# Inverting the softmax sums in three sets of chunks, and storing the last attention output in the final stage

## The chip, the cores and the metric

The kernel runs on one core of a Trainium2 chip. The metric is the device time of one execution in microseconds, as the median of several runs. Engines are named TensorE (PE in the profile, PEld for its weight loads), VectorE (DVE), ScalarE (ACT), GpSimd (POOL) and SyncE (SP). SPq, ACTq and POOLq are the DMAs that an engine issues.

## The reference

x has 2 sequences of 2048 tokens with 256 channels; everything is float32, with 16 heads of 16 channels.

```
x = x + attn_a(layernorm(x))   # 44 fixed offsets per token, local
x = x + ffn(layernorm(x))      # 8 groups of 512 tokens, each its own W1, b1, W2, b2
x = x + attn_b(layernorm(x))   # rotary positions, softmax over all 2048 tokens
x = x + ffn(layernorm(x))      # the same weights again

# attn_b, the part that the change touches
attn = softmax(einsum('bqhd,bkhd->bhqk', q, k) * DH ** -0.5)
out = einsum('bhqk,bkhd->bqhd', attn, v).reshape(b, l, d)
return out @ Wo
```

## The kernel before

The program has three stages, each a block of its own: all five engines have to arrive at the end of one before any goes on to the next. `local_stage` does attn_a, the first feed-forward and the projections of attn_b. `full_attention` does the softmax attention. `final_stage` does the output projection, the second feed-forward and the stores.

**full_attention** goes over 2 sequences, 4 groups of 4 heads and 4 query chunks of 512 tokens, 32 iterations in all (y = 0 to 31, chunks innermost). In each, TensorE makes the scores of 16 key tiles (L1270), ScalarE their exponentials (L1343), and TensorE weighs the values (L1279) into one PSUM bank: for each head 16 rows of unscaled output and one row with the sum of the exponentials. TensorE also makes the scores of the next iteration once more so that VectorE can take row maxima (L1241, L1357); the negated maxima go through SyncE into extra rows of the query tile (`neg_rows`, L1145), and TensorE waits for them at the start of an iteration. The last iteration has no next one, so VectorE has no work of this kind in it.

ScalarE copies the finished bank to the tile `ou` (`take_output`, L1333), a few exponentials into the next iteration. SyncE stores it with 8 DMAs (`output`, L1151 and L1152): per head 16 rows to `o_d`, and the row of sums to `s_d`. The softmax isn't divided here. That is done per chunk c of 512 tokens over all heads (c = 0 to 7; 0 to 3 are the first sequence, 4 to 7 the second; the last head group of the second sequence finishes chunks 4 to 7 in iterations 28 to 31):

- `load_totals` (L1046, 4 DMAs) and `load_outputs` (L1053, 4 DMAs) bring the sums and outputs of chunk c back to SBUF. GpSimd issues them for chunks 0 to 6 once the stores of that chunk have landed, and with them `load_rest` (x, the feed-forward's weights, a bias). Chunks 0 to 3 come while the last head group runs.
- `invert` (L1067): VectorE takes the reciprocals of the sums.
- `store_inverse` (L1073): SyncE stores them, 4 DMAs a chunk, to `r_d`.
- `load_inverse` (L1079): SyncE loads them again, each row spread over 16 partitions, 2 DMAs of 256 KB a chunk.
- `divide` (L1088): VectorE multiplies a chunk's output by them.

For chunks 0 to 6 the sums, outputs, inverse stores and inverse loads each have one semaphore, and its waits ask for all seven chunks. So VectorE inverts nothing until chunk 6's sums are there, SyncE loads nothing until all 28 stores have landed, and VectorE divides nothing until all 14 loads have. Divides 0 to 5 are the last of VectorE's work in the stage, divide 6 stands in the final stage. SyncE's order at the end of the stage is: output 30, stores of chunks 0 to 6, loads of chunks 0 to 6, output 31.

**final_stage** goes over the chunks. For each, TensorE projects (L1502), VectorE adds x (L1553), a layer norm follows in five steps over three engines (L1425 to L1466), then the feed-forward matmuls (L1512; its two layers were folded into one matrix earlier), VectorE's update (L1561) and ScalarE's store (L1537). SyncE fetches chunk 7 here: it waits for all outputs, then loads sums and outputs, stores and loads the inverse. VectorE inverts chunk 7 while it works on chunk 1 and divides it while it works on chunk 3.

## Time and profile before

| | us |
|---|---|
| median of 3 runs | 2459.34 |
| the runs | 2453.56, 2459.34, 2460.16 |
| the profiled execution's own time | 2459.12 |
| its span | 2457.4 |
| TensorE busy in the span | 2325.7 |
| VectorE busy | 1933.8 |
| ScalarE busy | 1590.6 |
| TensorE's mean granted clock | 0.978 of full speed |

Times in the trace count from the start of the span. The full attention runs from about 878 to 2345 us, the final stage from 2363 to the end. A fp32 matmul over 512 columns shows as two instructions. A line in the profile may be that of a helper that many places call (L1046 serves GpSimd and SyncE alike), so engine and tile have to be read with it; `ks` and `qs`, the key and query tiles, hold the chunks' buffers once attention no longer needs them. DMA issues aren't counted as busy time.

### The profile page before, as it was taken

Reading aid. Unit: us, or ns where it says so; the run is one execution under the profiler, and the core shown is the slowest. Engines: PE = TensorE matmul, PEld = TensorE weight load, DVE = VectorE, ACT = ScalarE, POOL = GpSimd, SP = SyncE. Lnnn points to the kernel's source line nnn. Section 1 sums busy time; section 2 is a strip of 40 time slices with the busy share of each in tenths; the row PEclk is TensorE's granted clock in tenths of the full one; section 3 lists DMA queues with packets and bytes.
Section 4 is the critical chain, followed back from the end, with each engine's and each line's share of the span. In section 5 each row is a group of like instructions: output and inputs, shape, how many; then the busy total and the mean of one; then the engine's idle time right before and its main releaser. Section 6 shows DMA issues by size and latency. Waiting matters only on the chain. (4 is left out here: it accounts for less than half of the span.)

```text
span 2457.4 us, 49260 instructions
## 1 busy us (share of the span) xinstructions
PE 2325.7 (95%) x14912; PEld 907.6 (37%) x14912; DVE 1933.8 (79%) x2283; ACT 1590.6 (65%) x3672; POOL 779.8 (32%) x1020
## 2 busy tenths in 40 slices
PE   7899999999987779999999999999999999999968
PEld 5455555555544322232323333333323232323223
DVE  4877988898867677888888888888888888888346
ACT  0356676766653156777777777777777777777821
POOL 2788988898871034020020020020000000041200
PEclk9999999999998799999999999999999999999989
DMA  8355545565566079050050050050000000030221
GB/s 268 114 130 126 159 119 151 136 152 136 149 139 151 14 133 107 7 71 3 4 71 3 4 71 4 3 71 4 3 20 5 2 20 5 2 108 27 64 98 52
DMA packets 246488, 178.42 MB, mean 73 GB/s; under 512 B 107238, under 2 KB 216118, under 8 KB 246374
## 3 DMA queue, kind: packets, MB, share of 16 engines
q1 hardware_dynamic: 210428, 114.37, 18.2%
q0 software_dynamic: 16480, 43.52, 11.3%
q10 hardware_dynamic: 19472, 19.12, 2.4%
q8 instruction: 63, 1.03, 0.2%
q14 instruction: 45, 0.37, 0.1%
HBM read 119.86 MB, written 48.31 MB: 68 GB/s over the span
## 5 line engine op out<-in xcount | busy, mean ns | idle before, releaser
L1343 ACT ACTIVATE pr<-ps_s 128x512 f32<-128x512 f32 x2048 | 1114.2, 598 | 338.5 <-PE ps_s L1270 314.4
L1357 DVE TENSOR_REDUCE mx<-ps_m 128x1 f32<-128x1024 f32 x980 | 1153.8, 1219 | 223.8 <-PE ps_m L1241 217.6
L1270 PE MATMUL ps_s<-qs,ks 99*128 (+1 forms) x2048 | 702.2, 383 | 20.2 <-SPq L1136 7.6
L1241 PE MATMUL ps_m<-ks,qs 96*128 (+1 forms) x1960 | 586.3, 380 | 0.0
L1279 PE MATMUL ps_o<-pr,vg 128*32 128x512 f32 x4096 | 546.3, 605 | 0.7 <-DMA vg<-vb_d 0.5
L541 POOL TENSOR_TENSOR qs<-ks 128x512 f32<-128x512 f32 x336 | 428.0, 1307 | 70.0 <-ACT ks L792 43.6
L1270 PEld LDWEIGHTS ps_s<-qs,ks 99*128 (+1 forms) x2048 | 195.6, 96 | 654.0 <-issue 429.6
L1184 POOL DMA_DIRECT2D vg<-vb_d x24 | 19.6, 817 | 1172.9 <-PE ps_o L1279 1085.0
L1241 PEld LDWEIGHTS ps_m<-ks,qs 96*128 (+1 forms) x1960 | 189.9, 98 | 173.6 <-issue 10.1
L871 DVE TENSOR_TENSOR ks<-PSa,ks 128x512 f32<-128x512 f32 x368 | 232.3, 677 | 22.6 <-PE PSa L626 20.4
L626 PE MATMUL PSa<-ks,sj 128*32 128x512 f32 x736 | 198.8, 608 | 4.7 <-issue 2.7
L626 PE MATMUL PSa<-qs,sj 128*32 128x512 f32 x672 | 198.7, 606 | 1.5 <-POOL qs L541 1.5
L1279 PEld LDWEIGHTS ps_o<-pr,vg 128*32 128x32 f32 x4096 | 80.6, 108 | 207.3 <-ACT pr L1343 155.6
L815 ACT ACTIVATE attn<-PSa,red 128x44 f32<-128x44 f32 x416 | 117.5, 314 | 6.4 <-DVE red L937 6.1
L822 ACT COPY qs<-PSa 128x512 f32<-128x512 f32 x128 | 69.4, 600 | 45.9 <-PE PSa L694 38.6
L815 ACT ACTIVATION_READ_ACCUMULATOR attn<-PSa,red 128x1 f32 x416 | 92.7, 223 | 0.0
L1177 POOL DMA_DIRECT2D qs<-q_d x168 | 85.6, 513 | 16.1 <-issue 5.1
L694 PE MATMUL PSa<-ident,qs 128*128 128x128 f32 x512 | 70.2, 281 | 12.9 <-DMA qs<-skew 9.6
L591 PE MATMUL PSa<-tail_room 128*128 128x256 f32 x256 | 65.5, 412 | 12.7 <-DMA tail_room<-in_W2T 9.3
L694 PEld LDWEIGHTS PSa<-ident,qs 128*128 128x128 f32 x512 | 57.7, 143 | 46.9 <-issue 35.7
L631 PE MATMUL PSa<-t_xm,wqkv_b 128*128 128x512 f32 x128 | 61.6, 626 | 5.5 <-DVE ks L977 5.0
L556 POOL TENSOR_TENSOR far<-far,fart 128x128 f32<-128x128 f32 x128 | 63.0, 492 | 10.0
(190 smaller groups left out, 2147.5 us busy)
## 6 DMA issues: line engine op xcount, KB each, us to landing
qs<-skew SPq DMA_DIRECT2D x64, 512.0 KB
ks<-k_d POOLq DMA_DIRECT2D x48, 256.0 KB, 8.9
qs<-q_d POOLq DMA_DIRECT2D x180, 64.0 KB, 9.1
skew<-attn SPq DMA_DIRECT2D x64, 164.0 KB, 4.7
tail_room<-in_W SPq DMA_DIRECT2D x32, 256.0 KB, 3.3
tail_room<-in_W2T SPq DMA_DIRECT2D x32, 256.0 KB, 4.1
vb_d<-vb SPq DMA_DIRECT2D x8, 1024.0 KB, 6.6
q_d<-qparts ACTq DMA_DIRECT2D x16, 384.0 KB, 2.7
```

The source lines that it names most:

```text
L541: pool.tensor_tensor(prod_p[:, n % RING, :], qT[:, c, :], kT[:, c, col:col + CH], ALU.mult).then_inc(prod_p_ready, 1)
L626: pe.matmul(PS[SLOT * g:SLOT * (g + 1), SC_BANK, :], sj[:, BANK_J * bank + 4 * g + r, :], rhs[:, n % RING, :], start=(r == 0), stop=(r == ...
L694: tr = pe.transpose(PS[:, TURN_BANK[half], h * P:(h + 1) * P], own[:, w % 2, 4 * half + h, :], ident[:, :])
L815: ex = act.activation(attn[:, w % 2, h, :], logits[:, h, :], ACT.Exp, bias=red[:, w % 2, 0, h:h + 1], accum_out=red[:, w % 2, 1, h:h + 1])
L822: act.copy(a0[:, 4 * half:4 * half + 4, :], PS[:, TURN_BANK[half], :].rearrange("p (h t) -> p h t", h=4)).then_inc(turn_sb, 1)
L871: dve.tensor_tensor(prod_d[:, n % RING, :], PS[:, Q_BANK[c], :], kT[:, c, col:col + CH], ALU.mult).then_inc(prod_d_ready, 1)
L1177: pool.dma_start(qs[r, bass.ds(g * NCH + n, 1), :, :].rearrange("p a j t -> p (a j) t"), D["q_d"][Q_STACK[i], :, heads, bass.ds(b * T + (1 ...
L1241: mm = pe.matmul(ps_m[:, u % 2, kc * CH:(kc + 1) * CH], qs[0:KROWS, bass.ds(nq, 1), j, qt * P:(qt + 1) * P].rearrange("p a t -> p (a t)"), ...
L1270: pe.matmul(ps_s[:, op % SB, :], ks[0:KROWS + PARTS, bass.ds(slot, 1), j, kt * P:(kt + 1) * P].rearrange("p a t -> p (a t)"), qs[0:KROWS + ...
L1279: mm = pe.matmul(ps_o[SLOT * j:SLOT * (j + 1), :], vg[:, kt, j, :], pr[:, kt % 4, j, :], start=(kt == 0), stop=(kt == KT - 1), skip_group_ ...
L1343: act.activation(pr[:, kt % 4, j, :], ps_s[:, op % SB, :], ACT.Exp, scale=HD ** -0.5).then_inc(p_ready, 1)
L1357: dve.tensor_reduce(mx[:, j * TILES + qt, half:half + 1], ps_m[:, u % 2, :], AX_X, ALU.max).then_inc(m_read, 1)
```

## The change

The chunks fall into three sets, 0 to 3, 4 to 6, and 7. Sums loaded, outputs loaded, inverses stored and inverses loaded have a semaphore for each set, and each wait asks for its own set. VectorE's order becomes: invert 0 to 3, divide 0 to 3, invert 4 to 6, divide 4 to 6, all in the attention stage; divide 6 is no longer in the final stage. SyncE's order becomes: the last `neg_rows`, stores of chunks 0 to 3, their loads, output 30, stores of chunks 4 to 6, their loads. Output 31 moves behind the stage boundary and is the first thing that SyncE does in the final stage. For that, `output` is now a function of the module, and `ou` and its semaphore are among the final buffers. GpSimd's program and the arithmetic are as before.

```diff
--- before.py
+++ after.py
@@ -998,6 +998,8 @@
 
 
 EARLY = 2
+SET_SIZE = (NCH, NCH - 1, 1)
+SET = [0] * NCH + [1] * (NCH - 1) + [2]
 
 
 def final_buffers(nc, ctx, A):
@@ -1009,6 +1011,7 @@
         "spread": sb("spread", [P, TILES, P]),
         "eps": sb("eps", [P, 1]),
         "wo": sb("wo", [P, KC, C]),
+        "ou": sb("ou", [P, CH]),
     }
     own = {
         "xc": sb("xc", [P, EARLY, KC, CH]),
@@ -1034,21 +1037,32 @@
         F["total"].append(own["total"][:, c] if c < EARLY else place(c % 2, P))
         F["inv"].append(place(c % 2, KC * CH).rearrange("p (k t) -> p k t", k=KC))
     F["bcc"] = [own["bcc"][:, c] for c in range(NG)]
-    for n in ("const_ld", "wo_ld", "filled", "total_ld", "o_ld", "last_total_ld", "last_o_ld", "x_ld", "inverse_ready", "inverse_stored",
-              "inverse_ld", "o_ready", "o_stored"):
+    for n in ("const_ld", "wo_ld", "filled", "x_ld", "inverse_ready", "o_ready", "o_sb", "o_stored"):
         F[n] = sem(n)
+    for n in ("total_ld", "o_ld", "inverse_stored", "inverse_ld"):
+        F[n] = [sem(n + str(k)) for k in range(len(SET_SIZE))]
     return F
 
 
+def output(sp, D, F, y):
+    ou = F["ou"]
+    sp.wait_ge(F["o_sb"], y + 1)
+    for j in range(GRP):
+        first = SLOT * j
+        sp.dma_start(D["o_d"][y, HD * j:HD * (j + 1), :], ou[first:first + HD, :]).then_inc(F["o_stored"], 16)
+        sp.dma_start(D["s_d"][y // (HG * NCH), y // NCH % HG, y % NCH, :, j, :],
+                     ou[first + HD:first + HD + 1, :].rearrange("p (q t) -> p q t", q=TILES)).then_inc(F["o_stored"], 16)
+
+
 def load_totals(eng, D, F, c):
-    loaded = F["total_ld"] if c < NG - 1 else F["last_total_ld"]
+    loaded = F["total_ld"][SET[c]]
     for q in range(TILES):
         eng.dma_start(F["total"][c][SLOT * q:SLOT * q + H, :], D["s_d"][c // NCH, :, c % NCH, q]).then_inc(loaded, 16)
 
 
 def load_outputs(eng, D, F, c):
     b, n = c // NCH, c % NCH
-    loaded = F["o_ld"] if c < NG - 1 else F["last_o_ld"]
+    loaded = F["o_ld"][SET[c]]
     for g in range(HG):
         eng.dma_start(F["oT"][c][64 * (g % 2):64 * (g % 2) + 64, g // 2, :], D["o_d"][(b * HG + g) * NCH + n]).then_inc(loaded, 16)
 
@@ -1060,31 +1074,26 @@
 
 
 def invert(dve, F, c):
-    if c < NG - 1:
-        dve.wait_ge(F["total_ld"], 16 * TILES * (NG - 1))
-    else:
-        dve.wait_ge(F["last_total_ld"], 16 * TILES)
+    dve.wait_ge(F["total_ld"][SET[c]], 16 * TILES * SET_SIZE[SET[c]])
     dve.reciprocal(F["total"][c], F["total"][c]).then_inc(F["inverse_ready"], 1)
 
 
 def store_inverse(sp, D, F, c):
     sp.wait_ge(F["inverse_ready"], c + 1)
     for q in range(TILES):
-        sp.dma_start(D["r_d"][c, :, q * P:(q + 1) * P], F["total"][c][SLOT * q:SLOT * q + H, :]).then_inc(F["inverse_stored"], 16)
+        sp.dma_start(D["r_d"][c, :, q * P:(q + 1) * P], F["total"][c][SLOT * q:SLOT * q + H, :]).then_inc(F["inverse_stored"][SET[c]], 16)
 
 
 def load_inverse(sp, D, F, c):
+    sp.wait_ge(F["inverse_stored"][SET[c]], 16 * TILES * SET_SIZE[SET[c]])
     for k in range(KC):
         src = D["r_d"][c, 8 * k:8 * k + 8, :].unsqueeze(1).broadcast_to([8, HD, CH])
-        sp.dma_start(F["inv"][c][:, k, :], src).then_inc(F["inverse_ld"], 16)
+        sp.dma_start(F["inv"][c][:, k, :], src).then_inc(F["inverse_ld"][SET[c]], 16)
 
 
 def divide(dve, F, c):
-    dve.wait_ge(F["inverse_ld"], 16 * KC * (NG - 1 if c < NG - 1 else NG))
-    if c < NG - 1:
-        dve.wait_ge(F["o_ld"], 16 * HG * (NG - 1))
-    else:
-        dve.wait_ge(F["last_o_ld"], 16 * HG)
+    dve.wait_ge(F["inverse_ld"][SET[c]], 16 * KC * SET_SIZE[SET[c]])
+    dve.wait_ge(F["o_ld"][SET[c]], 16 * HG * SET_SIZE[SET[c]])
     dve.tensor_tensor(F["oT"][c], F["oT"][c], F["inv"][c], ALU.mult).then_inc(F["o_ready"], 1)
 
 
@@ -1114,13 +1123,12 @@
         vg = sb("vg", [P, KT, GRP, SLOT], F32)
         pr = sb("pr", [P, 4, GRP, CH], F32)
         mx = sb("mx", [P, GRP * TILES, HALVES], F32)
-        ou = sb("ou", [P, CH], F32)
         q0_ld, first_max = sem("c_q0_ld"), sem("c_first_max")
         (qk_ld, qk_ready, va_ld, vb_ld, vc_ld, s_ps, p_ready, pv_done, m_ps, m_read, nm_step,
-         nmp_ready, nmt_ps, nmt_sb, neg_ld, o_sb) = (sem("c_" + n) for n in (
+         nmp_ready, nmt_ps, nmt_sb, neg_ld) = (sem("c_" + n) for n in (
              "qk_ld", "qk_ready", "va_ld", "vb_ld", "vc_ld", "s_ps", "p_ready", "pv_done", "m_ps",
-             "m_read", "nm_step", "nmp_ready", "nmt_ps", "nmt_sb", "neg_ld", "o_sb"))
-        o_stored = F["o_stored"]
+             "m_read", "nm_step", "nmp_ready", "nmt_ps", "nmt_sb", "neg_ld"))
+        ou, o_sb, o_stored = F["ou"], F["o_sb"], F["o_stored"]
         block = ctx.enter_context(nc.Block())
 
         def unit_place(u):
@@ -1144,25 +1152,19 @@
                 sp.wait_ge(nmt_sb, y + 1)
                 sp.dma_start(qs[KROWS:KROWS + PARTS, y % (HG * NCH), :, :].rearrange("a j t -> a (j t)"), nmt[:, :]).then_inc(neg_ld, 16)
 
-            def output(y):
-                sp.wait_ge(o_sb, y + 1)
-                for j in range(GRP):
-                    first = SLOT * j
-                    sp.dma_start(D["o_d"][y, HD * j:HD * (j + 1), :], ou[first:first + HD, :]).then_inc(o_stored, 16)
-                    sp.dma_start(D["s_d"][y // (HG * NCH), y // NCH % HG, y % NCH, :, j, :],
-                                 ou[first + HD:first + HD + 1, :].rearrange("p (q t) -> p q t", q=TILES)).then_inc(o_stored, 16)
-
             neg_rows(1)
             for x in range(2, ITERS):
-                output(x - 2)
+                output(sp, D, F, x - 2)
                 neg_rows(x)
-            output(ITERS - 2)
-            for c in range(NG - 1):
+            for c in range(NCH):
                 store_inverse(sp, D, F, c)
-            sp.wait_ge(F["inverse_stored"], 16 * TILES * (NG - 1))
-            for c in range(NG - 1):
+            for c in range(NCH):
                 load_inverse(sp, D, F, c)
-            output(ITERS - 1)
+            output(sp, D, F, ITERS - 2)
+            for c in range(NCH, NG - 1):
+                store_inverse(sp, D, F, c)
+            for c in range(NCH, NG - 1):
+                load_inverse(sp, D, F, c)
 
         @block.gpsimd
         def _(pool):
@@ -1401,10 +1403,11 @@
             with dve.Fori(2, ITERS - 1) as x:
                 iteration(x)
             iteration(ITERS - 1, last=True)
-            for c in range(NG - 1):
-                invert(dve, F, c)
-            for c in range(NG - 2):
-                divide(dve, F, c)
+            for chunks in (range(NCH), range(NCH, NG - 1)):
+                for c in chunks:
+                    invert(dve, F, c)
+                for c in chunks:
+                    divide(dve, F, c)
 
 
 class LayerNorm:
@@ -1482,11 +1485,11 @@
 
         @block.sync
         def _(sp):
+            output(sp, D, F, BATCH * HG * NCH - 1)
             sp.wait_ge(F["o_stored"], 16 * 8 * BATCH * HG * NCH)
             load_totals(sp, D, F, last)
             load_outputs(sp, D, F, last)
             store_inverse(sp, D, F, last)
-            sp.wait_ge(F["inverse_stored"], 16 * TILES * NG)
             load_inverse(sp, D, F, last)
             sp.wait_ge(stored, 16 * KC * NG)
 
@@ -1569,8 +1572,6 @@
                 if c:
                     update(c - 1, 0)
                     update(c - 1, 1)
-                if c == 0:
-                    divide(dve, F, last - 1)
                 if c == 1:
                     invert(dve, F, last)
                 if c == 3:
```

## Rows read from the trace of the kernel before

**Rows 1.** The page: its span, and the group of attention's score matmuls (part 5).
```profile
span 2457.4 us, 49260 instructions
...
L1270 PE MATMUL ps_s<-qs,ks 99*128 (+1 forms) x2048 | 702.2, 383 | 20.2 <-SPq L1136 7.6
```

**Rows 2.** The waits from 2290 to 2458 us: engine, line, released by: total us, times, longest.
```profile
DVE f_oT L1088 <- DMA ks<-r_d: 32.4, 1, 32.4
```

**Rows 3.** Timeline of the seam: start us, us, engine, line, operation, tiles, count [idle before].
```profile
2342.30 2.21 PE L1279 MATMUL ps_o<-pr,vg 128*32 128x512 f32 x16
...
2344.58 0.59 ACT L1333 COPY ou<-ps_o 128x512 f32<-128x512 f32 x1 [1.19 <-PE ps_o L1279]
...
2355.89 1.23 DVE L1088 TENSOR_TENSOR f_oT<-f_oT,ks 128x1024 f32<-128x1024 f32 x1 [32.37 <-DMA ks<-r_d]
...
2361.57 1.22 DVE L1088 TENSOR_TENSOR qs<-qs 128x1024 f32<-128x1024 f32 x1
...
2363.08 2.73 SPq L1046 DMA_DIRECT2D qs<-s_d  x4
...
2363.27 5.57 PE L1502 MATMUL PSf<-f_oT,f_wo 128*128 128x512 f32 x8 [18.75 <-PEq L1107]
```

**Rows 4.** The chain that ended last: start us, us, what.
```profile
2363.27 5.59 PE PSf L1502 x8
...
2377.34 1.72 PE PSf L1502 x4
...
2384.33 0.86 DVE qs L1067
...
2454.21 0.75 DVE qs L1561
```

**Rows 5.** Timeline of GpSimd, VectorE and SyncE, 2200 to 2342 us (SPq: SyncE's DMA issues).
```profile
2200.60 0.75 POOL L1059 DMA_DIRECT2D f_bcc<-bc_d  x1
...
2292.49 0.22 DVE L1381 COPY nmt<-ps_s 48x128 bf16<-48x128 bf16 x1 [1.66 <-PE ps_s L1250]
...
2308.19 0.31 SPq L1151 DMA_DIRECT2D o_d<-ou  x1
...
2311.93 0.59 SPq L1152 DMA_DIRECT2D s_d<-ou  x1
...
2313.87 2.33 POOL L1046 DMA_DIRECT2D ks<-s_d  x4 [34.77 <-DMA s_d<-ou]
...
2317.70 1.76 DVE L1067 RECIPROCAL f_total<-f_total 128x128 f32<-128x128 f32 x2 [24.99 <-DMA ks<-s_d]
...
2318.68 5.39 SPq L1073 DMA_DIRECT2D r_d<-f_total  x8
...
2331.51 1.82 SPq L1073 DMA_DIRECT2D r_d<-ks  x4
...
2334.41 1.35 SPq L1079 DMA_DIRECT2D ks<-r_d  x2
...
2339.99 1.23 SPq L1079 DMA_DIRECT2D ks<-r_d  x2
```

**Rows 6.** Windows of 1 us: length, PE, PEld, DVE, ACT, POOL busy, PEclk, DMA share, GB/s.
```profile
2345.00:2346.00 1.00, 0.00 (x0) 0.00 (x0) 0.00 (x0) 0.17 (x1) 0.00 (x0) 1.00 0.51 199
...
2347.00:2348.00 1.00, 0.00 (x0) 0.00 (x0) 0.00 (x0) 0.00 (x0) 0.00 (x0) 0.50 0.55 209
...
2367.00:2368.00 1.00, 1.00 (x4) 0.52 (x3) 0.69 (x1) 0.00 (x0) 0.00 (x0) 0.95 0.66 158
```

**Rows 7.** Timeline early in attention, SyncE's queue and TensorE.
```profile
959.35 0.80 SPq L1145 DMA_DIRECT2D qs<-nmt  x1
...
976.01 0.61 PE L1270 MATMUL ps_s<-qs,ks 99*128 x1 [4.58 <-DMA qs<-nmt]
```

**Rows 8.** Timeline of VectorE in chunk 0 of the final stage.
```profile
2372.72 1.22 DVE L1088 TENSOR_TENSOR ks<-ks 128x1024 f32<-128x1024 f32 x1
...
2375.17 0.95 DVE L1455 RECIPROCAL f_rs<-f_sd 128x128 f32<-128x128 f32 x1 [1.24 <-ACT f_sd L1451]
```

## The prediction

> **What bounds the kernel now.** I began at the page's span [rows 1] and went to the place of the change, the seam between the attention stage and the final stage. Over the whole program TensorE sets the pace, but at the seam it does nothing. Of the waits of the last 170 us, VectorE's longest is the one on the inverse loads, ahead of the first divide [rows 2]. The timeline of the seam [rows 3] gives the order. TensorE's last attention matmul ends at 2344.51 and ScalarE's copy of the last output at 2344.58 + 0.59 = 2345.17. The first divide starts only at 2355.89, six of them run back to back, and the last ends at 2361.57 + 1.22 = 2362.79. SyncE's first issue of the final stage is at 2363.08 and TensorE's first matmul at 2363.27, so the stage boundary costs 0.29 to 0.48 us after the last engine arrives, and the last to arrive is VectorE, 17.62 us after ScalarE. Nothing of the final stage can start sooner, since its code lies behind the boundary. What ends last here is the load of the seven broadcast inverses.
>
> **What follows the seam** is one chain to the end, by the chain of work that ended last [rows 4]: eight projection matmuls in 5.59 us, then about 10 us a chunk, and the last update ends at 2454.96. It starts with the first projection, so a start x us sooner is an end x us sooner, as long as no later step has a due time of its own. The last chunk has one, and it is looked at below.
>
> **The change, part by part.** It removes no arithmetic: 7 inversions, 28 stores, 14 loads and 7 divides stay ahead of chunk 7's own. What changes is what waits for what.
>
> *Chunks 0 to 3 go first.* Their sums were already loaded: GpSimd issued the last load of chunk 3 at 2200.60 [rows 5]. VectorE's last attention instruction ends at 2292.49 + 0.22 = 2292.71, and after it VectorE idled 24.99 us until chunk 6's sums came [rows 5]. Now four inversions run from 2292.75, 0.88 us each (1.76 for two), done by 2296.3. They hide under the attention of the last query chunk. SyncE has nothing between its load of the last maxima, right behind 2292.71, and the output store at 2308.19, so it takes up the 16 stores at about 2293.7. One store costs 1.82 / 4 = 0.455 us in the row at 2331.51, and 5.39 / 8 = 0.67 us in the row at 2318.68, where GpSimd's loads of x and weights ran beside it. Nothing of that runs here, so I take 0.455: 7.3 us, to 2301.0. From the end of the last store before (2333.33) to the first load (2334.41) is 1.08 us. The eight loads start near 2302.1. Before, the ninth load was issued at 2339.99, 5.58 us after the first, so the eight are issued by 2307.7, just ahead of the output at 2308.19. Landing is slower than issue: fourteen loads went from 2334.41 to 2355.89, 1.53 us each. Eight need 12.3 us, to 2314.4; with the slow stores it would be 2318.
>
> *What is queued behind them.* On SyncE's queue it is the store of output 30, whose landing lets GpSimd load chunk 6's sums. Before, it was issued from 2308.19 to 2312.52 and seen landed at 2313.87, 1.35 us later. Now eight loads stand ahead of it. Below: no delay, as the issue is hardly touched. Above: it lands only 1.35 us behind the last load, at 2315.8 with the quick stores and 2319.4 with the slow ones. I take 2315.8, 1.9 us late. The Trainium skill, in "DMA: Bandwidth & Descriptors", section "Queues, rings and completion order", says that each DMA engine consumes its descriptors of one queue in ring order. By that rule the late end holds; the other end would need small stores to overtake. No row before shows these stores behind these loads with a landing to read.
>
> *Chunks 4 to 6.* VectorE's first four divides (about 1.14 us apart [rows 3]) end near 2319.0. The sums of chunk 6 took 2317.70 - 2313.87 = 3.83 us from GpSimd's first issue to the inversion, so the inversions start at 2319.6, and the first store at 2320.6. Twelve stores: the first eight at the slow 5.39 us (the x loads again), four at 1.82, to 2327.8; 1.1 us of landing; six loads at 1.53 = 9.2 us from 2328.9, to 2338.1; three divides 3.5 us, to 2341.6. That is 3.6 us inside ScalarE's 2345.17. At the upper ends (output 30 at 2319.4, 12 stores at 0.67, 1 us more for six loads, which show no steady state) it is 2341.6 + 3.6 + 0.8 + 1.0 = 2347.0, 1.8 us outside. So this part costs 0 on the path, at worst 1.8, and it is where the cover is thin: each further us costs a us.
>
> *The seam then.* The last to arrive is ScalarE's copy, at 2345.17. TensorE starts 0.48 us later, at 2345.65 in place of 2363.27: **17.62 us** sooner.
>
> *The clock.* The first eight projection matmuls took 5.59 us at the seam and take 2 x 1.72 = 3.44 once the stage runs [rows 4]. The granted clock was still 1.00 between 2345 and 2346, more than half a us into TensorE's idle time, and 0.50 (1.2 GHz) between 2347 and 2348; it came back to 2.4 GHz between 2367 and 2368 [rows 6]. The gap now is 2345.65 - 2344.51 = 1.14 us. The other side: an idle of 4.58 us early in attention was followed by a score matmul of 0.61 us, where the mean of that group is 0.383 [rows 1, 7], so a gap of that size does lose it. 1.14 us lies nearer the stretch that kept it. I take the whole **2.15 us**; the lower end is 0.
>
> *The divide of chunk 6* leaves the final stage. It ran from 2372.72 to 2373.94, and the next VectorE instruction waited for ScalarE until 2375.17 anyway [rows 8]. Worth 0.
>
> *The last output* is stored behind the boundary. Before, SyncE issued it inside the attention stage; now it does so from about 2345.5, eight in 4.33 us as for output 30 [rows 5], to 2349.8; landed 1.35 later; its sums loaded 3.8 us after that, near 2355. Who waits is the inversion of chunk 7 on VectorE, with chunk 1's normalisation behind it. Its place was 2384.33, 21.06 us after the first matmul [rows 4]; now 18.9 us after 2345.65, at 2364.6. So 9 us of slack, price 0. What comes after it (store, load, divide two chunks later) keeps its distances.
>
> Sum: 17.62 + 2.15 = 19.8 us, against the profiled execution's own 2459.12 us (0.2 below the median of the runs shown, 2459.34): **2439.4 us**, 0.8% less.
>
> **The rivals.**
> 1. *The second set is late.* VectorE still arrives last, on chunk 6's divide. For it: a chain of four transfers with 3.6 us of cover. Against: most of its lengths are read from rows with the same traffic. Price 1 to 2 us, with a few us more if the six loads crawl: 2441 to 2445, 2442 as its middle.
> 2. *The clock is lost all the same,* or TensorE's first instructions behind the boundary aren't at hand when it comes straight from work. For it: before, TensorE had waited 18 us there, so the trace can't show it. Price 2.15: 2441.6.
> 3. *The other side: output 30 stuck behind the first set's loads.* In a full DMA system a small load by SyncE, issued at 959.35, held TensorE until 976.01, 16.7 us instead of one or two [rows 7]. If output 30 landed 16.7 us after its last issue, at 2329.2, that is 13.4 us behind my 2315.8, the divides end at 2355.0, the gap loses the clock, and it gives 2459.1 - (2362.8 - 2355.0) = 2451.3. It is slower only if the landing is over 21 us behind mine. Against it: then GpSimd's queue was full, here the loads are SyncE's own and end by 2318.
> 4. *Chunk 7's chain bounds.* From 9 us of slack it would have to be some 29 us late to undo the gain. Near nothing.
>
> **How the numbers follow.** The forecast as summed 0.68, rival 1 0.16, rival 2 0.09, rival 3 0.05 (half of it ending at no change or worse), rival 4 0.02. The measure tells a change from none at about 0.3%, 7.4 us. The forecast and rivals 1 and 2 are all faster, and so is part of rival 3: faster 0.95, within 0.02, slower 0.03. Range: above, 2444 takes in rival 1 and rivals 1 and 2 together; below, 2435, since one run of three was 5.8 us under the median, and the stall of 4.58 us in [rows 7], which hangs on how transfers meet, may be absent from some executions.
>
> **What would show it.** Right: VectorE's inversions of chunks 0 to 3 at 2293 to 2296; SyncE's first loads near 2302; GpSimd's load of chunk 6's sums near 2316; the last divide ending before ScalarE's last copy; TensorE's gap at the seam about 1.1 us, granted clock 1.00 across it, the first projection at about 3.4 us; no wait at chunk 7's inversion. Wrong: the last divide behind the copy (rival 1, the excess is the price), a first projection over 5 us (rival 2), GpSimd's load of the sums after 2320 (rival 3). Attention itself must keep its length; if its tail stretches under the earlier transfers, that comes off the gain.

## The result, and the profile after

The changed kernel took 2440.74 us (median of 4 runs, 2439.34 to 2441.76) against 2457.12 us for the one before (4 runs, 2453.56 to 2460.16): ratio 0.9933, interval [0.9916, 0.9951], 0.7% faster. The forecast was 2439.4, in a range of 2435 to 2444. The profiled execution took 2439.34 us, as good as the forecast; but it came to that sum by other terms, and the larger part of this text is about them.

The page of the changed kernel, its span, beside [rows 1]:

```profile
span 2437.7 us, 49260 instructions
```

Its seam in the timeline, beside [rows 3]:

```profile
2337.75 0.61 PE L1281 MATMUL ps_o<-pr,vg 128*32 128x512 f32 x4
...
2338.43 0.59 ACT L1335 COPY f_ou<-ps_o 128x512 f32<-128x512 f32 x1 [1.19 <-PE ps_o L1281]
...
2339.91 1.22 DVE L1097 TENSOR_TENSOR ks<-ks 128x1024 f32<-128x1024 f32 x1
...
2341.42 0.32 SPq L1052 DMA_DIRECT2D o_d<-f_ou  x1
...
2341.60 5.27 PE L1505 MATMUL PSf<-f_oT,f_wo 128*128 128x512 f32 x8 [3.23 <-PEq L1116]
```

Read it from the middle: ScalarE's copy ends at 2338.43 + 0.59 = 2339.02. VectorE's last divide ends at 2341.13, 2.11 us behind it (it was 17.62 behind), and TensorE starts at 2341.60, 0.47 us after that divide. So from the copy to the first projection it is 2.58 us in place of 18.10: 15.5 us gained, not 17.6. The last to arrive is still VectorE.

The steps that lead to that divide, beside [rows 5] (same view, 2286 to 2338 us):

```profile
2286.49 1.75 DVE L1078 RECIPROCAL f_total<-f_total 128x128 f32<-128x128 f32 x2
...
2293.70 2.01 SPq L1084 DMA_DIRECT2D r_d<-qs  x4
...
2297.38 1.39 SPq L1091 DMA_DIRECT2D ks<-r_d  x2
...
2306.93 0.58 SPq L1053 DMA_DIRECT2D s_d<-f_ou  x1
...
2311.47 1.23 DVE L1097 TENSOR_TENSOR f_oT<-f_oT,ks 128x1024 f32<-128x1024 f32 x1 [21.62 <-DMA qs<-r_d]
...
2312.55 2.33 POOL L1060 DMA_DIRECT2D ks<-s_d  x4 [39.56 <-DMA s_d<-f_ou]
...
2316.24 0.95 DVE L1078 RECIPROCAL ks<-ks 128x128 f32<-128x128 f32 x1
...
2317.23 1.71 SPq L1084 DMA_DIRECT2D r_d<-ks  x4
...
2320.84 1.94 SPq L1084 DMA_DIRECT2D r_d<-ks  x4
...
2326.84 1.31 SPq L1091 DMA_DIRECT2D ks<-r_d  x2
...
2337.63 1.23 DVE L1097 TENSOR_TENSOR ks<-ks 128x1024 f32<-128x1024 f32 x1 [18.81 <-DMA ks<-r_d]
```

Everything here counts best from ScalarE's copy, which carries no trace of what happened earlier. The table sets the forecast's times against these rows; before, the copy ended at 2345.17.

| us from ScalarE's last copy | forecast | measured |
|---|---|---|
| first set's first load | -43.1 | -41.6 |
| its loads landed, first divide | -30.8 | -27.6 |
| sums of chunk 6 asked for (output 30 landed) | -29.4 | -26.5 |
| inversions 4 to 6 start | -25.6 | -22.8 |
| second set's first load | -16.3 | -12.2 |
| its loads landed | -7.1 | -1.4 |
| last divide ends | -3.6 | +2.1 |

Attention itself kept its length: from the load of maxima issued at 1006.32 us (1012.26 before, both shown below) to the copy it is 1332.7 us, against 1332.9 before.

The six loads of the second set can be seen on the DMA engines too (windows of this execution; the last two figures are the engines' busy share and GB/s):

```profile
2327.50:2328.00 0.50, 0.50 (x6) 0.21 (x3) 0.00 (x0) 0.01 (x1) 0.00 (x0) 1.00 0.00 0
...
2329.00:2336.00 7.00, 6.23 (x37) 1.35 (x36) 0.00 (x0) 6.01 (x13) 0.00 (x0) 1.00 0.52 196
```

The first load is issued at 2326.84, nothing moves until 2328, then some 196 GB/s until about 2336, and the divide starts at 2337.63.

The granted clock, windows of 1 us (the third column from the right), beside [rows 6]:

```profile
2340.00:2341.00 1.00, 0.00 (x0) 0.00 (x0) 1.00 (x1) 0.00 (x0) 0.00 (x0) 1.00 0.00 0
...
2340.60:2341.60 1.00, 0.00 (x0) 0.03 (x1) 0.53 (x1) 0.00 (x0) 0.00 (x0) 0.91 0.00 0
...
2341.60:2342.60 1.00, 1.00 (x2) 0.48 (x3) 0.00 (x0) 0.00 (x0) 0.00 (x0) 0.50 0.15 33
...
2345.00:2346.00 1.00, 1.00 (x4) 0.52 (x3) 0.69 (x1) 0.00 (x0) 0.00 (x0) 1.00 0.14 29
...
2352.00:2353.00 1.00, 1.00 (x5) 0.50 (x2) 0.00 (x0) 0.99 (x2) 0.00 (x0) 0.50 0.74 225
```

TensorE's gap is 3.23 us. The clock is at full speed for most of it and falls to 1.2 GHz about 0.2 us before the first projection starts (windows of 0.25 us put the fall between 2341.25 and 2341.50), some 3 us behind the last attention matmul. It stays there, with TensorE busy, until just ahead of 2345, and falls again in chunk 0, ahead of 2352. In the chain that ended last, beside [rows 4], this reads so:

```profile
2341.60 5.29 PE PSf L1505 x8
...
2352.15 3.38 PE PSf L1505 x4
...
2427.85 6.54 PE PSf L1515 x8
...
2434.42 0.75 DVE qs L1564
```

The first projection takes 5.29 us, hardly less than the 5.59 before; the next one 3.38 in place of 1.72; the last feed 6.54, where the chain before had 5.41. From the first projection to the end of the last update it is 93.57 us, and it was 91.69. Beside this execution of the kernel before, what the clock was to give back (2.15 us) is a loss of 1.9. The first projection gives 0.3 us, and chunk 0 and the last feed lose 2.2; b will show that this stretch can be as long in the kernel before.

So 15.5 - 1.9 = 13.6 us at and behind the seam, and yet the two executions are 19.8 us apart. The other 6.2 us lie 1330 us earlier, where nothing was changed. SyncE's loads of the maxima early in attention, of the changed kernel:

```profile
959.69 0.80 SPq L1153 DMA_DIRECT2D qs<-nmt  x1
...
1006.32 0.80 SPq L1153 DMA_DIRECT2D qs<-nmt  x1
```

and of the kernel before:

```profile
1012.26 0.80 SPq L1145 DMA_DIRECT2D qs<-nmt  x1
```

Before, the load that follows the one at 959.35 [rows 7] was issued 52.91 us behind it; here the distance is 46.63 us, 6.28 less. TensorE's wait of 4.58 us, and the slow matmuls behind it, are absent. Whether that belongs to the change or to the execution was the first thing to settle.

### The profile page after: what moved, and what is told of

It reads as the page before. It is cut to its first block and busy times, and to the rows that moved or that the text cites. A ratio compares the mean times of both kernels' runs of the same rounds, so it can differ in the third digit from the quotient of the medians.

```text
span 2437.7 us, 49260 instructions
## 1 busy us (share of the span) xinstructions
PE 2330.2 (96%) x14912; PEld 910.8 (37%) x14912; DVE 1934.9 (79%) x2283; ACT 1590.0 (65%) x3672; POOL 780.5 (32%) x1020
## 3 DMA queue, kind: packets, MB, share of 16 engines
q8 instruction: 63, 1.03, 0.2%
## 5 line engine op out<-in xcount | busy, mean ns | idle before, releaser
L822 ACT COPY qs<-PSa 128x512 f32<-128x512 f32 x128 | 69.3, 601 | 45.8 <-PE PSa L694 39.4
L694 PE MATMUL PSa<-ident,qs 128*128 128x128 f32 x512 | 69.7, 280 | 12.6 <-DMA qs<-skew 8.7
```

Of the source, the lines that this page charges most:

```text
L694: tr = pe.transpose(PS[:, TURN_BANK[half], h * P:(h + 1) * P], own[:, w % 2, 4 * half + h, :], ident[:, :])
L822: act.copy(a0[:, 4 * half:4 * half + 4, :], PS[:, TURN_BANK[half], :].rearrange("p (h t) -> p h t", h=4)).then_inc(turn_sb, 1)
```

## The experiments

Each kernel was profiled once and timed beside the kernel before, in 5 to 12 runs. Kernels of one group (a to d, e to h, i to l) share the runs of before, whose medians were 2456.35, 2456.16 and 2454.77 us. The ratio follows the means and not the medians, so the two can disagree. Times "from the copy" are read from each profile as above.

### a. The changed kernel again

> The changed kernel once more, to part what the change does from what the start of attention does. In the two profiled executions the start differs by 6.3 us (a 4.58 us wait of TensorE for the maxima's load, and slow matmuls behind it, only in the one of before), and the rest of the difference is 13.6 us (18.10 to 2.58 us from ScalarE's last copy to the first projection, less 1.88 us from there to the end). Theory: the gain of the change is 13.6 us (ratio 0.9945), and the medians' 16.4 us hold part of the start's luck. Rival: the change also shortens the start, as it moves tiles; then the ratio is 0.992 or lower and the wait is never seen in this kernel.

Median 2438.55 us, ratio 0.993 [0.9915, 0.9946]. The start: 47.24 us between the two maxima loads, a wait of 1.2 us. So the changed kernel has that wait too, short here. The seam:

```profile
2340.18 2.21 PE L1281 MATMUL ps_o<-pr,vg 128*32 128x512 f32 x16
...
2342.70 1.22 DVE L1097 TENSOR_TENSOR ks<-ks 128x1024 f32<-128x1024 f32 x1
...
2344.39 5.37 PE L1505 MATMUL PSf<-f_oT,f_wo 128*128 128x512 f32 x8 [2.00 <-PEq L1116]
```

The divide ends at 2343.92, 0.88 us behind the copy (2343.04): how late VectorE is depends on the execution, since the loads do (12.9 us for the first set here, 14.1 in the other profile). TensorE's gap is 2.0 us, and here the windows show the clock falling after work has begun again (at 2344.39):

```profile
2343.00:2344.00 1.00, 0.00 (x0) 0.00 (x0) 0.92 (x1) 0.04 (x1) 0.00 (x0) 1.00 0.00 0
...
2344.00:2345.00 1.00, 0.61 (x1) 0.30 (x2) 0.00 (x0) 0.00 (x0) 0.00 (x0) 0.86 0.00 0
...
2345.00:2346.00 1.00, 1.00 (x3) 0.44 (x2) 0.00 (x0) 0.00 (x0) 0.00 (x0) 0.50 0.24 51
```

A gap of 2.0 us is enough to lose it, and here it isn't paid in the gap. The ratio, 0.993 twice, lies between the two that were to be told apart, and the intervals hold both. The rows decide: the changed kernel has the wait too.

### b. The kernel before again

> The kernel before against itself. Theory: its executions fall into two groups, about 2454 and about 2460 us, by whether the maxima's load issued near 959 us lands late behind GpSimd's key and query loads; the ratio is 1 within its interval, and a profile near 2454 us shows no wait of TensorE there. Rival: the 6 us lie elsewhere, and a fast execution still shows the 4.6 us wait.

Ratio 1.0001 [0.999, 1.0011]; 12 runs from 2450.29 to 2457.84 us with no gap between them, so the two groups that I expected don't show. The profile, of an execution of 2453.78 us, has 46.76 us between the two maxima loads, and none of TensorE's longest waits is on them: the kernel before doesn't always have the late load. Its seam, in one row:

```profile
2354.68 1.22 DVE L1088 TENSOR_TENSOR qs<-qs 128x1024 f32<-128x1024 f32 x1
```

The last divide ends at 2355.90, 17.19 us behind the copy (2338.71), and the first projection starts 17.67 us behind it. The stretch behind the seam took 93.24 us (93.28 in j); 91.69 was on the short side. Chunk 1's projection, which runs inside chunk 0's layer norm, took 3.08 us here, as slow as in the changed kernel.

### c. Divides 4 to 6 in the final stage

```diff
-            for chunks in (range(NCH), range(NCH, NG - 1)):
-                for c in chunks:
-                    invert(dve, F, c)
-                for c in chunks:
-                    divide(dve, F, c)
+            for c in range(NCH):
+                invert(dve, F, c)
+            for c in range(NCH):
+                divide(dve, F, c)
+            for c in range(NCH, NG - 1):
+                invert(dve, F, c)
...
                     update(c - 1, 1)
+                if c < 3:
+                    divide(dve, F, NCH + c)
```

> The changed kernel, with the divides of chunks 4, 5 and 6 moved into the final stage (while chunks 0, 1 and 2 are worked on). Theory: at the boundary VectorE, 2.11 us behind ScalarE's last copy, is what ends the attention stage, and the gap of 3.24 us costs the clock another 1.85 us in the first projection. Then ScalarE's copy ends the stage, TensorE starts 0.48 us behind it (2.1 us sooner), the first projection takes 3.4 to 3.5 us, and chunks 1 and 2 pay 1.1 and 0.4 us for the divides: 2.4 us faster than the changed kernel, up to 4 if the second slow stretch in chunk 0 goes too. Rival: the boundary or TensorE's first instructions need some 2.5 us from ScalarE's copy whoever is last, and the move only adds its 1.5 us.

Median 2437.11 us, ratio 0.9924 [0.9904, 0.9944]; against a it is 1.4 us less and not resolved. The profile resolves it:

```profile
2339.16 0.59 ACT L1335 COPY f_ou<-ps_o 128x512 f32<-128x512 f32 x1 [1.18 <-PE ps_o L1281]
...
2340.20 3.67 PE L1506 MATMUL PSf<-f_oT,f_wo 128*128 128x512 f32 x8 [1.11 <-PEq L1116]
```

ScalarE's copy (ends 2339.75) is last, TensorE is 0.45 us behind it with a gap of 1.11 us, the clock holds and the projection takes 3.67 us. Nothing at the boundary needs 2.5 us of its own; the rival falls. The final stage pays in chunks 1 and 2 for the divides: 92.20 us behind the seam. From the copy to the end it is 92.65 us, against 96.15 in the changed kernel's first profile and 95.25 in its second.

### d. TensorE kept busy up to the boundary

```diff
             weigh(KT - 1, ITERS * SCORES)
+            pe.wait_ge(m_read, ITERS * MAXU)
+            for _ in range(12):
+                pe.matmul(ps_m[:, 0, 0:CH], ks[0:KROWS, HG - 1, 0, 0:P], qs[0:KROWS, HG * NCH - 1, 0, :], start=True, stop=True)
```

> The changed kernel, with 12 more bf16 matmuls of 512 columns on TensorE behind the last attention matmul, into a bank that nobody reads; about 0.22 us each, so 2.6 us that end just before VectorE's last divide does. Theory: the first projection's 5.29 us is the granted clock's fall in the gap of 3.24 us; with the gap filled it is 3.44 us, the start stays where it is, and the kernel is 1.85 us faster, up to 3.4 with the slow projection of chunk 0 (3.45 in place of 1.98). Rival: the first matmuls behind the boundary are slow for another reason (operands, weights, instructions); then they stay at 5.3 us and the time is unchanged.

Median 2434.18 us, ratio 0.9928 [0.9906, 0.995]: four runs lie from 2431 to 2435 us and two at 2443 and 2444, so the median is 4.4 us under a's and the ratio is a's. The times don't resolve it; the profile, of a run of 2433.01 us, is read for the mechanism.

```profile
2334.88 2.76 PE L1329 MATMUL ps_m<-qs,ks 96*128 96x512 bf16 x12
...
2335.99 1.22 DVE L1097 TENSOR_TENSOR ks<-ks 128x1024 f32<-128x1024 f32 x1
...
2338.09 3.67 PE L1508 MATMUL PSf<-f_oT,f_wo 128*128 128x512 f32 x8 [0.45 <-PEq L1116]
```

VectorE is late as in the changed kernel (its last divide ends at 2337.21, 1.61 us behind the copy), the first projection starts 2.49 us behind the copy, and yet it takes 3.67 us: with 2.76 us of matmuls in the gap the clock stays up, in chunk 0 too. The added matmuls end at 2337.64, 0.43 us behind the divide, so here TensorE itself is last at the boundary, and not VectorE. From the first projection to the end it is 90.73 us in place of 93.57 and 93.90. Of these 2.8 to 3.2 us, 2.6 to 2.8 lie ahead of chunk 7: the clock at the seam and in chunk 0. The slow stretch at the end (chunk 7) was still there.

### e. Output 31 back in the attention stage

```diff
             for c in range(NCH, NG - 1):
                 load_inverse(sp, D, F, c)
+            output(sp, D, F, ITERS - 1)
...
-            output(sp, D, F, BATCH * HG * NCH - 1)
```

> The changed kernel with one part undone: output 31 is stored at the end of the attention stage again, behind the inverse loads. Theory: its 8 issues take 4.5 us from 0.3 us behind ScalarE's copy, so SyncE arrives at the boundary 4.8 us behind the copy in place of VectorE's 2.1, TensorE's first projection starts 2.6 to 2.7 us later, and the kernel is 2.6 us slower than the changed one. Rival: the issue is hidden behind VectorE's divides (the chain of the second set is the only bound), and the time is unchanged.

Median 2442.9 us, ratio 0.9932 [0.9909, 0.9956].

```profile
2336.83 0.58 ACT L1336 COPY f_ou<-ps_o 128x512 f32<-128x512 f32 x1 [1.19 <-PE ps_o L1282]
...
2338.01 1.22 DVE L1097 TENSOR_TENSOR ks<-ks 128x1024 f32<-128x1024 f32 x1
...
2341.20 0.58 SPq L1053 DMA_DIRECT2D s_d<-f_ou  x1
...
2342.73 5.35 PE L1505 MATMUL PSf<-f_oT,f_wo 128*128 128x512 f32 x8 [5.97 <-PEq L1116]
```

The divide ends at 2339.23 and no longer counts; SyncE's last issue ends at 2341.78, 4.37 us behind the copy, and the first projection comes at 5.32, 2.7 us later than in the changed kernel. With the loads as short as this, the eight small stores are the bound. The times don't resolve the 2.7 us: the ratio is that of the changed kernel (0.9933 and 0.993), and the runs spread from 2437 to 2445 us.

### f. x, weights and bias loaded early

```diff
                 load_outputs(pool, D, F, c)
-                load_rest(pool, D, F, c)
-            load_rest(pool, D, F, NG - 1)
+                if c < NCH:
+                    load_rest(pool, D, F, c)
+                if c == NCH - 1:
+                    for late in range(NCH, NG):
+                        load_rest(pool, D, F, late)
```

> The changed kernel, with GpSimd's loads of x, weights and bias of chunks 4 to 7 issued with those of chunks 0 to 3, before it waits for chunk 4's outputs. The sums and outputs of a chunk are loaded as before. Theory: the second set is late because the stores of its inverses needed 4.06 us from the last issue to landing, beside GpSimd's x loads, against 1.67 for the first set. Without that traffic they need about 1.7, VectorE's last divide ends 2.4 us sooner, about with ScalarE's copy, the gap is 1.1 to 1.4 us, and the kernel is 2.1 us faster, or 4 if the clock holds. Rival: the 4.06 us come from something else in the second set (its loads' fixed part, the queue); then the last divide stays 2.1 us behind the copy.

Median 2436.4 us, ratio 0.9909 [0.9885, 0.9934].

```profile
2317.85 1.81 SPq L1084 DMA_DIRECT2D r_d<-ks  x4
...
2320.69 1.31 SPq L1091 DMA_DIRECT2D ks<-r_d  x2
...
2334.09 1.22 DVE L1097 TENSOR_TENSOR ks<-ks 128x1024 f32<-128x1024 f32 x1
...
2336.45 3.67 PE L1508 MATMUL PSf<-f_oT,f_wo 128*128 128x512 f32 x8 [1.11 <-PEq L1116]
```

From the end of the second set's stores (2319.66) to the first load it is 1.03 us. In the changed kernel it was 4.06 and in its repeat 3.12, and in the three other kernels with early x loads (g, i, l) 1.04 each time. The divide ends 0.68 us before the copy, TensorE's gap is 1.11 us and the projection takes 3.67 us. From the copy to the end it is 91.94 us, 3.3 to 4.2 less than in the changed kernel's two profiles; the intervals of the times overlap.

### g. Both

> The changed kernel with both edits: x, weights and bias early, and divides 4 to 6 in the final stage. Theory: ScalarE's copy is last at the boundary already with the late divides alone, so the early x loads add nothing at the seam; as fast as the late divides alone within 0.5 us. Rival: it adds up to 2 us more, if the x loads also delay something in the last iteration of attention.

Median 2436.22 us, ratio 0.9906 [0.9881, 0.9931], beside 0.9909 for f. At the seam 0.46 us from the copy and a projection of 3.67 us, as in c and f; behind it 92.18 us, as in c. The two edits buy the same thing, and the late divides charge for it (92.18 us against 91.48 in f).

### h. The kernel before, with group 3's loads held back

```diff
             for g in range(1, 4):
+                if g == 3:
+                    pool.wait_ge(pv_done, 3 * KT)
                 load_qk(0, g, g)
```

> The kernel before (not the changed one), with GpSimd's key and query loads of head group 3 held back until three key tiles past iteration 1's start have been weighed. Theory: the wait at the start of attention is iteration 2's maxima load standing behind those loads on the DMA engines; with fewer of them in flight it lands in 2 us, TensorE's wait of 4.6 us and the slow matmuls behind it are gone in every execution, and all runs are near 2454 us: 0 to 6 us faster than before, by how many runs of before had the wait. Rival: held back, they collide with the next maxima load in place of this one, and the wait moves by one iteration or grows.

Median 2452.33 us, ratio 0.9977 [0.9961, 0.9993]: 2 to 10 us faster, where 0 to 6 was expected. The two maxima loads stand 45.82 us apart, as everywhere later in attention (about 45.8), and TensorE doesn't wait for them. But the runs still spread over 12.3 us, 2447.7 to 2460.0 (b's spread over 7.6, those of before beside it over 19.7), so they are not all near 2454. This execution, one of the longest, had the first projection 22.45 us behind the copy: the fourteen loads took 26.7 us, where they took 21.5 in [rows 3, 5]. They moved 153 GB/s (2330 to 2353 us) where those of the kernel before moved 204 (2337 to 2354), at the same busy share of the DMA engines, 0.54. So the old seam itself varied by some 5 us with the speed of these loads.

### i. Idle places of two layer norms filled

In the final stage of f, TensorE gets 6 and 5 matmuls ahead of the mean and the variance of chunk 0, and 8 and 5 ahead of `back` and `feed` of chunk 7, each on constant tiles and into a free bank.

```diff
+            def busy(n, bank):
+                for _ in range(n):
+                    pe.matmul(PS[:, bank, :], F["ones"].bitcast(BF16)[:, 0:P],
+                              F["spread"][:, :, :].rearrange("p q t -> p (q t)").bitcast(BF16)[:, 0:CH], start=True, stop=True)
```

> The changed kernel with x, weights and bias loaded early (as in the kernel named f), and matmuls that nobody reads in TensorE's idle places of the layer norms of chunk 0 (6 and 5 of them) and chunk 7 (8 and 5), about 0.22 us each, less than the idle times of 1.51, 1.44, 2.01 and 1.31 us that they stand in. Theory: the granted clock also falls in these chains: the projection of chunk 1 took 3.08 us in f and 1.98 at full clock, the last feed 6.32 and 3.44. With them bridged the stretch from the first projection to the last update shrinks from 91.5 us in f to about 87.5, and the kernel is 3 to 4 us faster than f. Rival: the falls do not hang on these idle places, or the matmuls stand in the way of the real ones; then the stretch stays at 91 to 93.

Median 2438.78 us, ratio 0.9925 [0.9908, 0.9943]: not the gain over f that was expected. The profile shows both halves. In this execution the second set's loads were slow (12.5 us for six, from 2327.75 to 2340.24; 10.8 in the changed kernel), VectorE came 2.2 us behind the copy, the gap was 3.33 us and the first projection took 6.52 us. Behind that projection all was at full clock: the projection of chunk 1 took 1.98 us, the last feed 3.71 (6.33 in f). The stretch was 90.95 us, or 88.1 without the 2.85 us of the slow start. For chunk 7 that is clear, since all twelve profiles without the added matmuls have its last feed at 5.28 to 6.79 us. For chunk 0 it isn't: the projection of chunk 1 is at full clock in before, c, d and g too, with the same two waits unfilled.

### j. Output 31 alone

The kernel before, with only `output(ITERS - 1)` moved to the head of SyncE's final stage (and `ou` with it).

> The kernel before with one part of the change alone: output 31 stored in the final stage, all seven chunks still one set. Theory: the seam is bound by the fourteen loads and the divides behind them, so the part alone is worth nothing (the time of before within 1 us; the seam 17.7 to 18.1 us as before). Rival: the eight small stores at the end of the load queue delay the last loads or the boundary; then the seam shrinks by 1 to 2 us.

Median 2456.37 us, ratio 1.0005 [0.9992, 1.0018]: alone the move is worth nothing.

```profile
2363.89 1.22 DVE L1099 TENSOR_TENSOR qs<-qs 128x1024 f32<-128x1024 f32 x1
...
2365.58 2.90 PE L1512 MATMUL PSf<-f_oT,f_wo 128*128 128x512 f32 x3 [17.39 <-PEq L1118]
```

The last divide still comes last (2365.11, 16.26 us behind the copy at 2348.85). The seam is 16.73 us, 0.9 to 1.4 less than in the two profiles of before, which is the rival's size; the fourteen loads took 20.9 us against 21.5 and 21.7, and one profile can't tell the edit from the execution. In this execution the start of attention had 56.58 us between the two maxima loads, 10.8 more than need be. As `ou` stands here where the changed kernel has it, that move doesn't take the late load away.

### k. Output 30 ahead of the first set's loads

```diff
+            output(sp, D, F, ITERS - 2)
             for c in range(NCH):
                 load_inverse(sp, D, F, c)
-            output(sp, D, F, ITERS - 2)
```

> The changed kernel with output 30 issued ahead of the first set's eight loads. Theory: output 30 landed 1.08 us behind the last of these loads, 4.6 us after its own last issue, since it stood behind them; ahead of them it lands 1.35 us after its last issue, so GpSimd's load of chunk 6's sums comes about 30.2 us before ScalarE's last copy in place of 26.5. But the loads of the first set begin only at about 31.5 us before the copy and land 14 us later, VectorE's divides 0 to 3 stand ahead of the inversions 4 to 6, and the second set is late: the last divide ends some 11 to 13 us behind the copy, and the kernel is 9 to 12 us slower than the changed one. Rival: output 30's landing is set by the small stores themselves; then GpSimd's load stays near 26.5 us ahead.

Median 2455.96 us, ratio 1.0001 [0.9988, 1.0014]: the whole gain is gone.

```profile
2306.83 0.60 SPq L1053 DMA_DIRECT2D s_d<-f_ou  x1
...
2307.47 1.32 SPq L1091 DMA_DIRECT2D ks<-r_d  x2
...
2308.77 2.32 POOL L1060 DMA_DIRECT2D ks<-s_d  x4 [35.17 <-DMA s_d<-f_ou]
...
2329.82 1.23 DVE L1097 TENSOR_TENSOR f_oT<-f_oT,ks 128x1024 f32<-128x1024 f32 x1 [38.96 <-DMA qs<-r_d]
```

Output 30, issued until 2307.43, has landed at 2308.77, 1.34 us later; behind the loads, in the changed kernel, it took 5.04 (2307.51 to 2312.55). So its landing is set by what stands ahead of it on SyncE's queue. The Trainium skill, in "DMA: Bandwidth & Descriptors", section "Queues, rings and completion order", says that each DMA engine consumes its descriptors in ring order, and the trace agrees. But the eight loads now take 22.4 us, not the 14 I had put in, and the last divide ends 16.4 us behind the copy in place of 11 to 13. GpSimd's x and weight loads, issued from 2313.15 to 2317.5, fall into them: the DMA engines are busy to 0.77 or more from 2314 to 2324, where the changed kernel has 0.4 to 0.65 under these eight loads. That this is the cause is read from these rows; no run has this order without GpSimd's traffic.

### l. All that helped

f, i's matmuls and h's wait in one kernel.

> The bridged kernel i with, beside it, GpSimd's key and query loads of head group 3 held back at the start of attention. Theory: the start's wait for the second maxima load (0.6 to 1.2 us in the changed kernel's profiles, 4.6 in one of before) is gone, and this kernel is 0.5 to 1 us faster than i in the usual execution and loses the slow ones. Rival: the start doesn't matter in most executions, and the two are equal within their spread.

Median 2430.7 us (2429.1 to 2433.76), ratio 0.9899 [0.9883, 0.9916]: the fastest of all, 24 us under before's 2454.77 and 8 us under i. Only the start differs from i by design; there it saves 1.3 us (45.84 us between the maxima loads, 47.13 in i). Of the 10.3 us between the two profiled spans, another 1.9 us lie at the seam and 2.85 in the first projection. The second set's six loads were as slow here (12.6 us) as in i (12.5), so it isn't they: i's first set took 14.6 us for its eight, this one 13.2, which is most of the 1.9 us. TensorE's gap is 1.45 us here, and the clock is kept. About 4 us stand before attention begins (SyncE's maxima load of iteration 0 at 867.5 and 871.7); no edit is there, and its cause stays open. So of the 8 us between the medians the rows give the edit only 1.3; 0.5 to 1 was expected of it. The chain behind the seam, three pieces of it:

```profile
2336.81 3.69 PE PSf L1515 x8
...
2420.42 3.71 PE PSf L1525 x8
...
2424.16 0.75 DVE qs L1582
```

The first projection takes 3.69 us, the last feed 3.71, and the stretch 88.10 us in place of 93.57.

## Why the prediction was right, and where it wasn't

**What bounds the seam, and that the gain is the wait for the loads: right.** The three sets took VectorE's arrival from 17.2 to 17.6 us behind the copy to 0.9 to 2.1. Output 31 alone gives nothing in the times (j); without it the rest loses 2.7 us at the seam of one profile (e), which the times don't resolve.

**"Chunks 4 to 6", 3.6 us inside: wrong.** The last divide came 2.1 us behind the copy, 5.7 us off and past even the 1.8 us of the upper end (0.9 in a, inside it). The miss has three terms. Loads: I divided 21.5 us by fourteen and used 1.53 us a load. But eight took 14.1 us and six 10.8. Between six and fourteen that is 1.34 a load over a fixed 2.8 us. The windows above show both: 256 KB at 196 GB/s are 1.34 us, and next to nothing moves in the first 1.2 us behind the first issue or in the last us ahead of the divide. Each set pays that anew. I had spread it over the fourteen, which cost 1.8 us in the first set and 1.6 in the second. The figures are of one execution each; six loads took 10.3 to 12.6 us in all, always more than my 9.2. Stores: the first set's took 8.3 us to issue in place of 7.3 (the first eight cost 0.54 each with no GpSimd traffic beside them) and 1.67 to land in place of 1.08. Of the 3.2 us by which the first set's loads landed late, 2.8 reach the second set's inversions. Traffic: I made the second set's stores slow to issue, beside GpSimd's x loads (7.2 us). They were quick to issue (5.6 us) and slow to land, 4.06 us, 1.3 us more in all. f took that traffic away, and the landing fell to 1.03 us. What was named as rival 1, VectorE still last, is what happened, 2.1 and 0.9 us late in the two profiles, against the 1 to 2 us that I gave for it.

**"The clock", 2.15 us: wrong.** I had reckoned with a gap of 1.14 us, and such a gap keeps the clock (1.11 us in c and f, 3.67 us for the projection). But VectorE's 2.1 us made the gap 3.2, and that loses it. The size was wrong too: I took 3.44 us for a projection at full clock, and it takes 3.67 to 3.69 (c, d, f, g, l), so against 5.59 there were 1.9 us to win. The two terms weren't independent, and my chances treated them as if they were: rival 1 carries rival 2 with it. d shows the clock's part by itself, 2.6 to 2.8 us with chunk 0.

**Output 30 and chunk 7: right in kind.** Output 30 landed 1.1 us behind the last load ahead of it, as I had taken it; against the copy that is 4.8 us later than before and not 1.9, through the later start and the length of those loads. Chunk 7's inversion never waited.

**The sum.** 17.62 + 2.15 = 19.8 us was forecast. The rows show 15.5 at the seam (16.3 between the repeats a and b) less 1.9 (0.7) behind it: 13.6 to 15.7. The medians show 16.4 and 17.8, with intervals from 12 to 21 us. The first profile's 19.8 us is 13.6 and 6.2 of luck at the start, which the forecast's number shared, as it was summed against an execution that had the wait. The number was within 1.3 us of the median; the working deserved to be 4 to 6 us off, so that is luck. The medians lie 1 to 3 us above the rows, and two things seen here could fill that. The old seam is sometimes longer: h's, 22.45 us, would make the gain at the seam 20 to 21 us. And the start's late load is sometimes long: 52.91 and 56.58 us between the maxima loads in before and j, 45.8 to 47.2 in the other twelve profiles, ten of which carry the sets. That the change itself shortens the start is unlikely: k has the changed kernel's start and a seam of 16.87 us, and its time is that of before within 3.4 us. The runs don't settle more than that.

## What to carry to other kernels

When a transfer of many pieces is cut into sets, time it as a fixed part for each set and a slope, taken from two rows of different counts; a mean over the whole hides the fixed part. Where the margin is a few us, take several executions of those rows: the same six loads differed by 2.3 us. When two terms hang on the same arrival (a wait, and the clock that falls in the wait), give them one chance, not two. And before a difference between two profiles is put down to a change, line both up at a mark near it, here ScalarE's last copy: the 6 us that weren't the change's became visible only so.

## What the runs showed of the hardware that wasn't expected

- TensorE's clock kept 2.4 GHz over gaps of 1.11 us (c, f, g) and 1.45 us (l) and lost it over 2.0 us (a) and 3.2 us. The moment differs: in a it fell 2.3 us behind the last matmul, when the next work had run for 0.3 us; in the changed kernel's first profile 3.0 us behind it, 0.2 us ahead of the next work; in before 2.1 us behind it. So a gap of 2.0 us is paid wholly behind itself: 5.4 us for the first projection in place of 3.7.
- It falls once more in chunk 7's layer norm, where TensorE waits 2.01 and 1.31 us: the last feed took 5.28 to 6.79 us in all twelve profiles that leave these waits empty, and 3.71 in the two that fill them. In chunk 0, with waits of 1.51 and 1.44 us and a matmul of 1.1 us between, it fell in eight of those twelve and not in before, c, d and g. In all, 24 idle-time matmuls of 0.22 us went with 3.4 us less in the stretch (91.48 in f, 88.10 in l).
- Twelve small stores (8 KB) beside GpSimd's 512 KB loads were issued at 0.43 to 0.46 us each, the last four at 0.45 to 0.71, and landed 2.7 to 4.1 us after the last, against 1.03 us without them. In the changed kernel that traffic ended at about 2325, 2 us before the stores were seen landed.
- The same six loads took 10.3 to 12.6 us in different executions, and the fourteen 20.9 to 26.7. The rate has two levels at the same busy share of the DMA engines (0.51 to 0.54): 189 to 204 GB/s in before, the changed kernel, a, b, d, e, f and j, 150 to 153 in h, i and l. What sets the level stays open.
